# Output products ahead of the next head's first scores on TensorE, in the attention of a fused decoder layer

## What is computed

```python
x = layernorm(x + attn(x, Wq, Wk, Wv, Wo))       # 32 query heads, 8 key/value heads of 64, rope, causal
x = layernorm(x + xattn(x, fside, ctx))          # two products quantized to 8 bits, silu gate
x = layernorm(x + ffn(x, up, down, scales))      # signs of the weights, relu, 512 -> 2048 -> 512

# in attn, for a batch and a query head:
attn = einsum('bkgqd,bkld->bkgql', qh, kh) * 64 ** -0.5
attn = where(causal, attn, -inf)
p = softmax(attn)
out = einsum('bkgql,bkld->bkgqd', p, vh)
return out @ Wo.T
```

## Time and profile before

| | us |
|---|---|
| median of 3 runs | 1482.75 (1481.66 to 1483.1) |
| the profiled execution | 1484.37 |
| its span, first to last instruction | 1482.6 |
| PE busy | 1313.8 (89%) |
| PE weight loads busy | 1081.3 (73%) |
| DVE busy | 998.1 (67%) |
| ACT busy | 940.2 (63%) |
| POOL busy | 751.6 (51%) |
| attention, from the first transposes to the last | 55.2 to 1155.8 |

### The profile page before, as it was taken

The page is one execution under the profiler, slowest core; times in us unless marked ns, Lnnn a source line. Parts: engine busy times, 40 slices in busy tenths (PEclk is TensorE's granted clock), DMA queues, the critical chain, the costliest instruction groups (busy, mean ns, idle before and its releaser), DMA issues.

```text
span 1482.6 us, 25047 instructions
## 1 busy us (share of the span) xinstructions
PE 1313.8 (89%) x7099; PEld 1081.3 (73%) x7112; DVE 998.1 (67%) x2435; ACT 940.2 (63%) x2197; POOL 751.6 (51%) x641
## 2 busy tenths in 40 slices
PE   3799999999999999898889888878897889899996
PEld 2588888888888877677777777767776667677775
DVE  3467777767777767878776786778777676744222
ACT  2576677676777776676767766666776584644332
POOL 3456555556556665465535464556441263536343
PEclk9799999999999999999999999999999999999999
DMA  4422212222122233222122222221235311010000
GB/s 170 147 75 65 58 50 67 64 78 60 50 61 58 72 89 100 72 64 58 50 62 76 58 51 58 79 57 47 52 86 162 139 37 49 18 40 3 26 29 28
DMA packets 54852, 98.78 MB, mean 67 GB/s; under 512 B 11744, under 2 KB 13792, under 8 KB 53728
## 3 DMA queue, kind: packets, MB, share of 16 engines
q1 hardware_dynamic: 54752, 97.57, 23.3%
HBM read 51.39 MB, written 4.19 MB: 37 GB/s over the span
## 4 chain that ended last, share of the span: by engine, by line
PE 63%; DVE 14%; ACT 10%; issue 7%; POOL 4%; DMA 1%; ACTq 0%; DVEq 0%; POOLq 0%; SPq 0%
PE m L1588 26%; PE ps_s L1588 8%; PE ps_o L1645 6%; PE ps_t L1633 6%; PE m L1873 6%; PE ps_s L1887 3%; PE ps_t L1887 3%; ACT pT_hi L1028 2%; DVE pT_lo L1308 2%; PE m L1655 2%; ACT probs L1020 2%; DVE o_sum L1261 1%; DVE probs L1247 1%; POOL y L963 1%; DVE sm_a L1361 1%
## 5 line engine op out<-in xcount | busy, mean ns | idle before, releaser
L1020 ACT ACTIVATE probs<-probs,neg_max 128x128 f32<-128x128 f32 (+3 forms) x512 | 285.2, 559 | 179.0 <-DVE neg_max L1247 178.4
L1308 DVE TENSOR_TENSOR pT_lo<-ps_t,pT_hi 128x512 fp32r<-128x512 f32 (+1 forms) x384 | 220.7, 595 | 148.0 <-ACT pT_hi L1028 145.8
L1633 PE MATMUL ps_t<-ident,probs 128*128 128x128 f32 x1280 | 188.3, 278 | 91.8 <-DVE pT_lo L1308 76.3
L1588 PE MATMUL ps_s<-k_st,q_st 128*128 128x256 f32 (+2 forms) x1024 | 236.0, 354 | 0.3 <-DVE neg_max L1247 0.3
L1633 PEld LDWEIGHTS ps_t<-ident,probs 128*128 128x128 f32 x1280 | 146.3, 142 | 122.4 <-DVE pT_lo L1308 94.8
L1247 DVE CUSTOM_DVE_ANT_0 probs<-ps_s,mask 128x128 f32<-128x128 f32 (+3 forms) x512 | 228.1, 482 | 6.8 <-PE ps_s L1588 6.6
L881 POOL TENSOR_TENSOR o_lo<-o_sum,o_hi 128x512 fp32r<-128x512 f32 x64 | 82.7, 1293 | 252.1 <-ACT o_hi L1042 252.1
L1028 ACT ACTIVATE pT_hi<-ps_t 128x512 fp32r<-128x512 f32 (+1 forms) x384 | 185.7, 518 | 5.6 <-PE ps_t L1633 2.5
L934 POOL TENSOR_TENSOR hid_lo<-hid,hid_hi 128x512 fp32r<-128x512 f32 x64 | 83.9, 1313 | 166.2 <-ACT hid_hi L1212 166.1
L1645 PE MATMUL ps_o<-pT_hi,v_st 128*128 128x256 f32 (+2 forms) x512 | 167.8, 339 | 0.0
L1588 PEld LDWEIGHTS ps_s<-k_st,q_st 128*128 128x128 f32 x1024 | 154.0, 195 | 4.0 <-DVE neg_max L1247 0.5
(11 more groups left out here) (251 smaller groups left out, 3064.9 us busy)
## 6 DMA issues: line engine op xcount, KB each, us to landing
q_st<-q_tmp SPq DMA_DIRECT2D x512, 64.0 KB, 2.0
raw<-in_wq_t SPq DMA_DIRECT2D x32, 256.0 KB, 3.0
k_st<-k_st SPq DMA_DIRECT2D x64, 128.0 KB, 2.4
raw<-in_wo_t SPq DMA_DIRECT2D x32, 256.0 KB, 3.0
raw_b<-in_ffn_t SPq DMA_DIRECT2D x10, 512.0 KB, 7.5
y<-in_x_t SPq DMA_DIRECT2D x4, 1024.0 KB, 10.8
raw<-in_wkv_t SPq DMA_DIRECT2D x16, 256.0 KB, 3.7
y<-in_x SPq DMA_DIRECT2D x4, 1024.0 KB, 5.7
```

Of the source, the lines that this page charges most:

```text
L1020: act.activation(probs[:, h % 2, SO[i]:SO[i] + SW[i]], probs[:, h % 2, SO[i]:SO[i] + SW[i]], ACT.Exp, bias=neg_max[:, h % 2, i:i + 1], sca ...
L1308: dve.tensor_tensor(pT_lo[:, d, :], ps_t[:, (h + k) % 2, 0:P * w].rearrange("p (w c) -> p w c", c=P), f32(pT_hi[:, d, :]), ALU.subtract).t ...
L1588: i = pe.matmul(dst, a, c, start=(j == 0), stop=(j == len(terms) - 1))
L1633: i = pe.transpose(ps_t[:, (h + k) % 2, P * c:P * (c + 1)], probs[:, h % 2, at:at + P], ident[:, :])
```

## The change

Two calls of `scores` move from ahead of the two calls of `project_out` to behind them. The conditions and all waits inside the calls stay as they are. Only TensorE's queue differs.

```diff
                         transpose_probs(n, h, 0)
                         transpose_probs(n, h, 1)
-                        if more:
-                            scores(*ahead, 0)
-                            scores(*ahead, 1)
                         if h == 0 and b != 1 and prev:
                             project_out(m1_fill(g, b, "out3"), u - 2, b % 2, 3)
                         if h > 0 and prev and (b, h) != (1, 1):
                             project_out(m1_fill(g, b, f"out{h - 1}"), u - 1, (b + 1) % 2, h - 1)
+                        if more:
+                            scores(*ahead, 0)
+                            scores(*ahead, 1)
                         transpose_probs(n, h, 2)
                         if more:
                             scores(*ahead, 2)
```

## The result

The changed kernel takes **1530.33 us** (median of 4 runs, 1528.7 to 1531.51) against 1482.44 (1481.66 to 1483.1) for the kernel before in the same runs: a ratio of **1.0322, 95% interval 1.0305 to 1.034**. The forecast was 1511, its range ended at 1528. The direction was right, the size was not: 48 us came where 28 were forecast. The profiled execution took 1531.51, its span 1529.7.

The account below looks back on a forecast made before the run. TensorE, 89% busy, was taken to set the pace in steps 1 to 7, with gaps already there from step 8. Terms 11.1 + 0 + 2 + 6.9 + 4.5 + 3.6 = 28.1 us gave 1511 us, range 1497 to 1528.

Parts of the forecast that it names:

- The maximum's start: Ordinary heads: VectorE's maximum starts 0.03 to 0.04 us after the scores' matmuls end, so 0.65 us later than now.
- the ordinary heads' 0.21: Cost per ordinary head on TensorE: 0.21 us, bounds 0 and 0.65; 53 heads make 11.1 us.
- The 0.34: Ordinary heads: the next scores' weights load 0.34 us after the maximum's start when they wait for it.
- The count: 92 places less 15 heads 1 of b = 0 and 24 others already waiting for `pT_lo`: 53 ordinary heads.
- the 24 with an earlier wait for `pT_lo`: Heads whose third transpose block already waits for `pT_lo`: nothing changes, 24 x 0 us, from 0 to 0.2 each.
- The bank m1: Reciprocals on TensorE wait for `add_y` to read their bank: 0.1 us in 20 heads, 2 us; bounds 0 and 0.3 each.
- The short heads: Head 1 of b = 0, 15 places: 1.15 us each in steps 1 to 6 (6.9), 0.5 each in 7 to 15 (4.5).
- Carried over: From step 8 on, VectorE's later work delays the late head behind an ordinary one: 8 x 0.45 = 3.6 us.
- D: Rival, faster, 1474 us: the product ends 0.48 us earlier, shrinking VectorE's 19 waits to add to `y`; chance 0.03.
- C: Rival, nothing, 1483 us: tile 2's scores are not late and the short heads have room; chance 0.03.
- A: Rival, short, 1497 us: delay mostly absorbed, 0.1 us per ordinary head, 0.6 per short one, 14 us; chance 0.14.
- B: Rival, long, 1530 us: VectorE's shift comes through, 0.4 per ordinary head, plus 8 us for the clock; chance 0.10.

Follow-up runs that it names:

- e4: The changed kernel without the separate semaphore instruction (`max_gate`) ahead of each maximum in steps 0 and 6 to 15; 1516.18 us against 1480.61 for the kernel before.
- e14: The changed kernel with the loop of steps 1 to 5 written out and `max_gate` left out everywhere; 1506.79 us against 1482.18 for the kernel before.
- e1: The kernel before with the change made only in heads 1 of b = 0 (15 places); 1490.49 us against 1481.81 for the kernel before.
- e2: The kernel before with the change made only in the 77 places other than heads 1 of b = 0; 1516.27 us, ratio 1.0233 to the kernel before.
- e3: The kernel before with only tile 1's scores moved behind the product, tile 0's left ahead; 1523.71 us against 1481.81 for the kernel before.
- e6: The kernel before with three of the product's six matmuls put ahead of the scores, three left behind; 1486.37 us against 1481.81 for the kernel before.

## Why the prediction was wrong in size

**The maximum's start.** The step that failed is "VectorE starts 0.03 to 0.04 us after a matmul's end [...], so the maximum starts at 437.26". The row it rests on is of an addition to `o_sum`, which carries its wait itself. In front of the maximum stands a separate instruction that does the waiting, and the mask starts 0.18 later still (0.22 in after, 0.04 in e4). That made the ordinary heads' 0.21 into 0.40 to 0.42, and in the loop, with the register instructions, into 0.47 to 0.53; the waits for `neg_max` are 103 of 0.30 us where 53 to 80 of 0.2 were forecast. The trace of before could have told: its list of waits has `probs <- ps_s` twice, 6.6 us, and the first one is the first maximum of the program.

```profile
45.99 0.82 PE L1588 MATMUL ps_s<-k_st,q_st 128*128 128x256 f32 x4
...
46.76 0.29 DVE L1247 CUSTOM_DVE_ANT_0 probs<-ps_s,mask 128x128 f32<-128x128 f32 x1 [6.11 <-PE ps_s L1588]
...
47.12 0.69 PEld L1588 LDWEIGHTS ps_s<-k_st,q_st 128*128 128x128 f32 x4 [0.51 <-DVE neg_max L1247]
```

The scores end at 46.81, tile 0's two by the same 0.24 at 46.57, and the maximum starts 0.19 later: this very wait, for the only time that it was exposed at tile 0, with its price. I took the row of another instruction from the head that I was working on.

**The 0.34** from the maximum's start to the next weights came out right (0.35), partly by luck. The row that it was read from does not show a wait for `neg_max`: these weights had loaded right behind those of the third transpose block, which had waited for `pT_lo` and ended at 469.53.

```profile
469.33 0.20 PEld L1633 LDWEIGHTS ps_t<-ident,probs 128*128 128x128 f32 x2 [0.88 <-DVE pT_lo L1308]
```

The measured distance stands in the row above, 46.76 to 47.12, again some 0.35, and there the weights did wait for `neg_max`.

**The count and the rest of that chain** were right: scores' end, the wait of the weights, heads without a product 0.00, ordinary heads in time cost. Of the 24 with an earlier wait for `pT_lo`, put at 0, those that had waited 0.76 us or more are mostly at 0.00 to 0.04 (two at -0.46 and -0.45, three at 0.9 to 3.1). But six had waited only 0.2 to 0.4 us, and they grew by 0.2 to 0.5, 2.1 us together: at so short a wait the place counts as one in time.

**The bank m1** was mis-sized: 0.1 each in 20 heads. e14 gives the term by itself as the heads with reciprocals less heads 3, 0.35 - 0.21 = 0.14; in the loop of after it is 0.2 to 0.27. The upper bound of 0.3 held.

**The short heads** (1.15 each) measured 1.40 to 1.47 in steps 1 to 6: the same 0.18 and the loop's instructions again. Without both it is 1.03 to 1.06, and 1.25 in step 6, so the reasoning through the exponentials held. The nine of steps 7 to 15, 0.5 each, measured 0.75 on average (1.0 in step 7, 6.0 in eight); e1 shows that part of it is given back in the heads behind.

**Carried over** (3.6 us for late heads) fell: most of those heads show nothing of it.

**The bounds.** The forecast's own bounds do not give the 1503 to 1521 that it states: with 53 heads at 0.15 to 0.3, six short ones at 0.8 to 1.3 and the rest as summed they give 1506 to 1517. The wider figure has no row behind it.

**Rivals.** D and C are out, A too. B's number, 1530, is the measured one by coincidence (39 in the heads and 8 for the clock, where 48 came in the heads and none by the clock), and its mechanism is half right: VectorE's delay does come through at `m1`, but its 0.4 per ordinary head came from the semaphore instruction, and its 8 us for the clock are not there (1.00 and 0.97 as before). 103 new gaps of at most 0.5 us left the clock where it was. By the Trainium skill, "TensorE: Matmul & The Clock Gate", section "A second HAM failure mode: psum-queue depth-cycling", frequent small gaps between groups of matmuls can cost clock; this trace shows none of that. The wait for `o_lo` grew from 5.6 to 12.9 us in 16 cases, 0.46 each: the scores' 0.48, and no loop behind it.

**By halves of the span**: of the forecast 28, 17 were for steps 0 to 7 (37 x 0.21, 2, 6 x 1.15 and 0.5), and 30.9 came; 11 were for steps 8 to 15, and 17.7 came. The first difference is accounted for head by head. The second is partly the same and partly head 0 of unit 28, the 3.05 that the last section takes up; how many of the other 1 to 2 us jumps there are of that kind was not tried.

## What to carry to other kernels

A group of matmuls between a tile and the next use of its bank is cover for the engine that empties the bank. In ordinary heads half of it was enough here, and none of it cost 3.2%; look how much each place needs, and give the surplus to places that have none (moving one product, and the copies that wait for it, made the kernel 1.7% faster; the product alone 0.6%). When an order is changed so that a wait becomes exposed, a waiting instruction that stands by itself ahead of the useful one becomes exposed too, and so can register instructions ahead of it: price the wait with a row of the same instruction when it last waited, not with that of a neighbour. And look which copies overwrite what a moved product reads, and what is queued behind them.

## What the runs showed of the hardware

A semaphore instruction of its own, ahead of a VectorE instruction, costs 0.18 us when it is the one that waits (0.22 against 0.04 from the matmul's end to the mask's start), and nothing when the wait was fulfilled long before.

VectorE's 128x512 `y<-y,mv,norm` takes 0.54 or 0.55 us in 13 of its 16 executions in before, and 1.5 to 2.7 in single ones beside GpSimd (1.51 and 2.08 in before; 1.52, 2.12 and 2.71 in after). The timeline of before, a piece of the second stage in head 0 of unit 28:

```profile
1012.83 2.76 POOL L942 TENSOR_TENSOR w_gu<-w_gu,cm 128x512 f32<-128x512 f32 x2
...
1013.76 2.70 DVE L1387 TENSOR_SCALAR y<-y,mv,norm 128x512 f32<-128x512 f32 x2 [0.15 <-DVE q_tmp L1227]
```

The same place in after:

```profile
1053.10 2.52 POOL L942 TENSOR_TENSOR w_gu<-w_gu,cm 128x512 f32<-128x512 f32 x2
1054.41 4.74 DVE L1387 TENSOR_SCALAR y<-y,mv,norm 128x512 f32<-128x512 f32 x2 [0.15 <-DVE q_tmp L1227]
...
1056.14 1.51 POOL L942 TENSOR_TENSOR w_gu<-w_gu,cm 128x512 f32<-128x512 f32 x1
1057.61 1.25 POOL L871 TENSOR_TENSOR wkvT_lo<-raw,wkvT_hi 128x512 fp32r<-128x512 f32 x1
```

The pair takes 2.70 us in before and 4.74 in after, since it came to stand beside other GpSimd instructions; in e4 it takes 2.56, and that head is 3.2 us shorter there. That is most of what head 0 of unit 28 lost. The other kernels go with it: where the pair takes 4.7 or 5.0 us (e2, e3) the head is 3.0 longer than before, where it takes 2.7 (e1, e6) it is as before. The Trainium skill, "SBUF — State Buffer", section "Who interferes with whom", says that VectorE in a two-port mode and GpSimd take a shared pair of ports in turn, and that the one that comes second is blocked until the other is done. The rows agree as far as they go: 2.1 and 2.7 us against 0.54, while other executions beside a GpSimd instruction keep their 0.54. Which mode the instruction runs in no run here shows. So a shift of a fraction of a microsecond can cost or give back 2 us in steps 8 to 15, where both engines are at work on the second stage.
